# Sort companions moved ahead of the folds, and six gather passes written out, in a graph network kernel

## The reference, cut to what matters

```python
def reference(x, src, dst, edge_type_16, edge_weight, ...):
    edge_index = jnp.stack([src, dst])
    # L0, three times: e = relu((x[dst]-x[src]) @ theta.T + x[src] @ phi.T); segment_max over src; batch norm; relu
    x = _layernorm(x + _L0_gnn_ref(x, src, dst, ...), axis=-1)
    # L1, twice: msg = (x @ W[type])[src] * edge_weight; mean over dst; + x @ root + bias; layer norm; relu
    x = _layernorm(x + _L1_gnn_ref(x, edge_index, edge_type_16, edge_weight, ...), axis=-1)
    # L2: (x @ W)[src] * norm, sum over dst; relu
    x = _layernorm(x + _L2_gnn_ref(x, edge_index, ...), axis=-1)
    # L3: attention along edges with a softmax over dst, then an MLP
    x = _layernorm(x + _L3_gnn_ref(x, src, dst, ...), axis=-1)
    return x
```

## Time and profile before

| | |
|---|---|
| time, median of 3 runs | 7478.22 us (7474.63 to 7485.05) |
| profiled execution | 7499.41 us, span 7497.7 us |
| busy, share of the span | VectorE 3766.1 us (50%), GpSimd 3180.5 (42%), TensorE 3015.6 (40%), ScalarE 1788.8 (24%) |
| moved by DMA | 1065.32 MB, mean 142 GB/s |
| mean granted TensorE clock | 0.691 |

### The profile page before, as it was taken

One profiled execution on the slowest core, in us unless ns is written; L12 is line 12 of the kernel. 1 busy time (PEld: TensorE's weight loads), 2 busy tenths in 40 slices (PEclk: granted clock), 3 DMA queues, 4 the chain that ended last, 5 costly groups with the idle time before them and its releaser, 6 DMA issues. The chain is left out here.

```text
span 7497.7 us, 64492 instructions
## 1 busy us (share of the span) xinstructions
PE 3015.6 (40%) x12777; PEld 1767.9 (24%) x12803; DVE 3766.1 (50%) x9366; ACT 1788.8 (24%) x4594; POOL 3180.5 (42%) x3188
## 2 busy tenths in 40 slices
PE   4373000433335445569700069400030005767748
PEld 3232000311113222234300024200020003555525
DVE  8995444344445455644445343333353335656553
ACT  1282000021112354521122222222220002333312
POOL 0003565434443555410266620366536663555540
PEclk9997555755556677779855579755565557888869
DMA  0003455323332444323355543455535553887840
GB/s 8 1 1 106 162 172 172 116 90 131 123 127 98 137 144 147 137 79 153 139 171 174 171 172 137 145 171 172 177 97 172 179 179 125 269 271 267 271 105 18
DMA packets 379809, 1065.32 MB, mean 142 GB/s; under 512 B 74258, under 2 KB 162612, under 8 KB 333012
## 3 DMA queue, kind: packets, MB, share of 16 engines
q0 software_dynamic: 164688, 466.32, 21.1%
q1 hardware_dynamic: 213586, 595.68, 21.0%
q10 hardware_dynamic: 1330, 0.99, 0.0%
HBM read 541.40 MB, written 521.29 MB: 142 GB/s over the span
## 5 line engine op out<-in xcount | busy, mean ns | idle before, releaser
L788 POOL DMA_INDIRECT out_of<-table,index x936 | 930.5, 994 | 1035.2 <-DVE index L812 756.2
L788 POOL DMA_INDIRECT rows<-table,index x728 | 719.5, 988 | 412.9 <-issue 229.6
L788 POOL DMA_INDIRECT rows<-typed_table,index x520 | 514.0, 988 | 684.4 <-DVE index L812 533.6
L3108 POOL DMA_INDIRECT qv<-qv_table,index x416 | 429.0, 1031 | 384.1 <-DVE index L3285 256.5
L788 POOL DMA_INDIRECT y<-typed_table,index x312 | 321.4, 1030 | 597.8 <-DVE index L812 504.8
L1493 PE MATMUL bank<-x,marks 128*128 128x416 f16 x1664 | 380.4, 386 | 418.9 <-ACT marks L1507 340.6
L827 DVE SCALAR_TENSOR_TENSOR y<-y,by_source_anew,out_of 128x256 f32<-128x256 f32 x897 | 434.0, 484 | 213.4 <-issue 89.4
L1507 ACT ACTIVATE marks<-hot_block,x 128x128 f16<-128x128 f16 x1248 | 370.9, 386 | 436.1 <-DVE marks L1548 430.3
L806 ACT ACTIVATE rows<-rows,by_target_weight 128x256 f32<-128x256 f32 x520 | 215.6, 494 | 611.2 <-DMA rows<-typed_table,index 586.8
L2157 PE MATMUL bank<-weights,turned_y 128*128 128x512 f32 x800 | 359.1, 598 | 5.5 <-ACT turned_y L2217 5.5
L1961 PE MATMUL bank<-weights,out_of 128*128 128x512 f32 x800 | 349.6, 595 | 13.2 <-DVE weights L2006 13.2
(11 more groups left out here) (586 smaller groups left out, 7605.4 us busy)
## 6 DMA issues: line engine op xcount, KB each, us to landing
states<-y SPq DMA_DIRECT2D x156, 1024.0 KB
typed_table<-staged SPq DMA_DIRECT2D x400, 256.0 KB, 2.0
states<-state SPq DMA_DIRECT2D x78, 1024.0 KB
states<-out_of SPq DMA_DIRECT2D x78, 1024.0 KB
wide_states<-y SPq DMA_DIRECT2D x52, 1088.0 KB
near<-k_rows SPq DMA_DIRECT2D x416, 128.0 KB
out_of<-table,index POOLq DMA_INDIRECT x936
rows<-table,index POOLq DMA_INDIRECT x728
```

Of the source, the lines that this page charges most:

```text
L788: pool.indirect_dma_start(out=rows[h][:, u * D:(u + 1) * D], out_offset=None, in_=table, in_offset=bass.IndirectOffsetOnAxis(ap=index[h][: ...
L3108: pool.indirect_dma_start(out=qv[b][:, u * PAIR:(u + 1) * PAIR], out_offset=None, in_=qv_table, in_offset=bass.IndirectOffsetOnAxis(ap=ind ...
```

## The change

- The loops of VectorE, ScalarE, TensorE and SyncE in `edge_pass`, `over_groups` and `Mixture` become Python loops: every group is its own code, slices and semaphore values are constants, and `held` goes. GpSimd's loop stays.
- Each companion has a `lead`: `CountTargets` and `PlaceTargets` 1, `MoveTargets` 3. VectorE does the companion's group g + lead behind `fold_group(g)`.
- `begin` gives the order of round 0: in pass 1 the four folds, the preparation, five companion groups; in pass 2 the settling with the four folds put between its parts, five groups; in pass 3 the preparation, three groups, and then a fold and a group in turn; in pass 6 the folds and then `ahead`, as before.
- `behind` stands before the last fold of the pass.

```diff
-                late = bool(beside) and beside.late
-                if beside and not late:
-                    dve.wait_ge(loaded, 16 * len(loads))
-                    beside.ahead(dve)
                 mixed_rounds = mixing.rounds if mixing else 1
+                if beside:
+                    beside.begin(dve, [lambda h=h: fold_group(0, h) for h in range(RING)])
+                else:
+                    for h in range(RING):
+                        fold_group(0, h, mix=bool(mixing))
+                for i in range(1, rounds - 1):
+                    for h in range(RING):
+                        fold_group(i, h, mix=i < mixed_rounds)
+                        beside_group(i, h)
                 for h in range(RING):
-                    fold_group(0, h, alone=late, mix=bool(mixing))
-                if late:
-                    beside.ahead(dve)
-                    for h in range(RING):
-                        beside.group(dve, h, h % 2)
-                if mixing:
-                    with dve.Fori(1, mixed_rounds) as i:
-                        for h in range(RING):
-                            fold_group(i, h, mix=True)
-                with dve.Fori(mixed_rounds, rounds - 1) as i:
-                    for h in range(RING):
-                        fold_group(i, h)
-                for h in range(RING):
+                    if beside and h == RING - 1:
+                        beside.behind(dve)
                     fold_group(rounds - 1, h, more=False)
+                    if beside and GROUPS - RING + h + beside.lead < GROUPS:
+                        beside_group(rounds - 1, h)
                 dve.wait_ge(chain, STEPS + 1)
                 nc.vector.tensor_copy(tail[:], state[RING - 1][:, (GROUP - 1) * D:])
-                if beside:
-                    beside.behind(dve)
...
-def over_groups(engine, body):
-    for h in range(2):
-        body(h, h)
-    with engine.Fori(1, GROUPS // 2 - 1) as i:
-        for h in range(2):
-            body(2 * i + h, h)
-    for h in range(2):
-        body(GROUPS - 2 + h, h)
+def over_groups(body):
+    for g in range(GROUPS):
+        body(g, g % 2)
...
+# MoveTargets
+    def begin(self, dve, folds):
+        self.ahead(dve)
+        for g in range(self.lead):
+            self.group(dve, g, g % 2)
+        for h, fold in enumerate(folds):
+            fold()
+            self.group(dve, h + self.lead, (h + self.lead) % 2)
...
+# PlaceTargets
+    def begin(self, dve, folds):
+        nc, order = self.sort.nc, self.sort.order
+        nc.vector.tensor_copy(self.run[0][:], order.start[:]).then_inc(self.running, 1)
+        self.settle.vector(dve, folds)
+        self.mask(dve, 0, 0)
+        for g in range(RING + self.lead):
+            self.group(dve, g, g % 2)
```

More of the change, by code:

```diff
@@ L799, in _ @@
                 def _(act):
-                    with act.Fori(0, rounds) as i:
+                    for i in range(rounds):
                         for h in range(RING):
                             act.wait_ge(gathered[h], (i + 1) * (16 * GROUP))
-                            act.sem_inc(held, 1)
                             for u in range(GROUP):
                                 row = rows[h][:, u * D:(u + 1) * D]
-                                nc.scalar.activation(row, row, ACT.Copy, scale=order.weight[:, bass.ds((RING * i + h) * GROUP + u, 1)]
+                                nc.scalar.activation(row, row, ACT.Copy, scale=order.weight[:, (RING * i + h) * GROUP + u:(RING * i + h) * GROUP + u + 1]
                                                      ).then_inc(weighed, 1)
@@ L831, in fold_group, with beside_group @@
                         look(g + RING, h)
-                    if beside and not alone:
-                        beside.group(dve, g, h % 2)
                     if mix:
                         mixing.group(dve, i, h)
+                def beside_group(i, h):
+                    if beside:
+                        beside.group(dve, RING * i + h + beside.lead, (h + beside.lead) % 2)
                 nc.vector.memset(state[RING - 1][:, (GROUP - 1) * D:], start).then_inc(chain, 1)
@@ L883, in _ @@
                     mixing.load(sp)
[L884 to L887, removed]
+                for i in range(rounds):
+                    store(i, mix=bool(mixing) and i < mixing.rounds)
                 if mixing:
@@ L1084 @@
 class CountTargets:
-    late = True
-    names = ("bits_made", "hot", "turned", "copied", "tallied", "summed", "totalled", "held")
+    lead = 1
+    names = ("bits_made", "hot", "turned", "copied", "tallied", "summed", "totalled")
     def __init__(self, sort):
@@ L1129, in body @@
                 act.wait_ge(turned, g + 1)
-                act.sem_inc(held, 1)
-                nc.scalar.copy(sort.z[:, bass.ds(g * P, P)], turn_bank[h][:, 0:P]).then_inc(copied, 1)
-            over_groups(act, body)
+                nc.scalar.copy(sort.z[:, g * P:(g + 1) * P], turn_bank[h][:, 0:P]).then_inc(copied, 1)
+            over_groups(body)
+    def begin(self, dve, folds):
+        for fold in folds:
+            fold()
+        self.ahead(dve)
+        for g in range(RING + self.lead):
+            self.group(dve, g, g % 2)
     def ahead(self, dve):
@@ L1214, in scalar, with vector @@
             nc.scalar.copy(order.end_row[:, b * BLOCK * P:b * BLOCK * P + block_width(b)], env.bank[2 + b % 2][:, 0:block_width(b)]).then_inc(self.kept, 1)
-    def vector(self, dve):
+    def vector(self, dve, folds):
         nc, env, order = self.sort.nc, self.sort.env, self.sort.order
+        first, second, third, fourth = folds
         n_blk, n_stp, l_blk, l_stp, end, crosses = self.n_blk, self.n_stp, self.l_blk, self.l_stp, self.end, self.crosses
@@ L1252, in vector @@
                                     op=ALU.mult).then_inc(self.masked_ends, 1)
+        second()
         dve.wait_ge(self.used, TILES)
@@ L1256, in vector @@
         nc.vector.tensor_scalar(out=self.ident_v, in0=env.ident[:], scalar1=self.open_all[:, 0:1], scalar2=None, op0=ALU.mult).then_inc(self.opened, 1)
+        third()
         dve.wait_ge(self.opened_row, 1)
         then(nc.vector.tensor_copy(order.open_row[:], env.bank[1][:, 0:P]))
+        fourth()
 class PlaceTargets:
-    late = True
+    lead = 1
     names = ("masked", "hot_tile", "alike", "compared", "code_met", "hot_block", "crossed", "hot_row", "tallied", "running", "added",
-             "cut_high", "cut", "looked_up", "picked", "placed", "ranked", "held") + SettleTargets.names
+             "cut_high", "cut", "looked_up", "picked", "placed", "ranked") + SettleTargets.names
     def __init__(self, sort):
@@ L1461 @@
 class MoveTargets:
-    late = False
-    names = ("step", "hot", "marked", "used", "held")
+    lead = 3
+    names = ("step", "hot", "marked", "used")
     def __init__(self, sort):
@@ L2032 @@
 class Mixture:
-    names = ("basis_loaded", "mixed", "filed", "mix_held")
+    names = ("basis_loaded", "mixed", "filed")
     rounds = TYPES // 2
@@ L2061, in group @@
             return
-        first = isinstance(c, int) and c == 0
+        first = c == 0
         if h == 0:
```

128 lines of the change are left out of this document (46 added, 82 removed).

## The result

| | before | after |
|---|---|---|
| median | 7476.43 us (7463.51 to 7485.05, 4 runs) | 7094.62 us (7038.82 to 7144.45, 4 runs) |
| ratio | | 0.9474 (95% interval 0.9438 to 0.9511) |
| profiled span | 7497.7 us | 7142.8 us |
| gathers with waits, passes 1 to 6 | 631, 854, 740, 648, 626, 615 us | 601, 690, 679, 589, 579, 596 us |
| GpSimd's waits in them | 95, 331, 189, 99, 91, 77 us | 51, 159, 109, 39, 42, 52 us |

What follows compares the result with a forecast made beforehand. GpSimd's row gathers, waiting 882 us in all mostly for VectorE's `index`, were taken to bound the kernel. Savings summed to 830 us, 7499 to 6669, set at about 6650 us for the median; 8 in 10 within 6550 to 7000.

Steps and rivals of the forecast that it cites:

- Loops written out: VectorE, ScalarE, TensorE, SyncE: register, branch and `held` instructions go, and with them the slow stretches returning each round.
- pass 1 and its end: Pass 1: waits fall from 95 to 17 us, saving 78; its last store comes 11 us sooner.
- pass 2 and its end: Pass 2: fewer waits save 261 us; no companions left over after the last gather saves 26.
- pass 3 and its end: Pass 3: stretch of 740 us falls to 576, saving 164; the next phase starts 46 us sooner.
- Passes 4 to 6: Last three passes: VectorE's groups well under GpSimd's 10.3 us, so waits nearly vanish, saving 96, 88 and 60 us.
- the first wait: Pass 2's first GpSimd wait, 61.9 us before: settling moved between folds leaves 40 us, bounds 15 to 62.
- the 553 taken: Pass 2's 416 gathers at 1.33 us each, gap included: 553 us.
- 10 us a group: Pass 3's companion through two buffers: 19 to 20 us for two groups, under GpSimd's pace by little.
- The ends: Ends of passes 1 to 3: `behind` before the last fold finds companions done, saving 11, 26 and 46 us.
- Rival B: Written-out code pays for its fetches, VectorE losing 30% of its time: 475 us saved, 7000 us; chance 0.19.
- Rival C: VectorE and GpSimd hinder each other: 2496 gathers each 0.11 us longer, 275 us, so 6925 us; chance 0.13.
- D: Slower than before: all written-out code at 0.70 us an instruction, pass 3's TensorE worst, about 9000 us; chance 0.04.

Runs made afterwards that it cites:

- experiment 6: The changed kernel, unchanged, run for its trace on a chip where the kernel before takes about 6355 us: 6366.05 us, ratio 1.0012.
- experiment 12: The changed kernel plus 24 one-column writes of zeros on VectorE per group in pass 6, on a slow chip: 7145.99 us, ratio 0.9548.
- experiment 5: The kernel before, unchanged, run for its trace on a quick chip: 6350.75 us.
- experiment 1: The kernel before with only the leads, the new round 0 order and the moved `behind`, all loops kept, on a quick chip: 6347.24 us, ratio 0.9983.
- experiment 14: The kernel before with only the loops written out, no lead and `behind` last, on a slow chip: ratio 0.9555.
- experiment 11: The changed kernel with a 128x866 write of zeros on VectorE ahead of each companion group in pass 1, on a slow chip: 7071.76 us, ratio 0.9431.

## Why the prediction was wrong

The mechanism was seen, its cure misjudged, and the gain that came was there on some chips only. **The step that failed is the first of "Loops written out": that the slow stretches go with the loops' register and branch instructions.** They come in straight code too, at the same 0.70 us, and cost 362 us of waits more than the 90 that the forecast left. Term by term, from the profiled executions:

| term | forecast | measured |
|---|---|---|
| pass 1 and its end | 78 + 11 | 30 - 10 |
| pass 2 and its end | 261 + 26 | 164 + 8 |
| pass 3 and its end | 164 + 46 | 61 + 17 |
| pass 4 | 96 | 59 |
| pass 5 | 88 | 47 |
| pass 6 | 60 | 18 |
| everything else | 0 | -39 |

The measured terms come to 355 us, the difference of the two profiled executions; the medians differ by 382.

- *Passes 4 to 6*: a fold went from 4.2 us to 0.7 or 1.4 us within the stretches, not to 0.52. That is 12.5 us a group, above GpSimd's 10.3.
- *Pass 2*: the first wait, taken as 40 us, is 43. Its gathers are 22 us less than the 553 taken (416 times 0.977 + 0.30 = 531); another 116 us of waits stayed.
- *Pass 3*: 10 us a group was about right where the supply is quick (groups 8 to 12 us apart); TensorE's slow stretches add a wait of 9 to 13 us ten times, 110 us.
- *The ends*: `behind` ahead of the last fold makes the last store wait for the companion, and the companion was late for the same reason. On the quick chip the stores lie 6 to 7 us behind the last gather, as forecast.
- *Rival B* had the mechanism, with 475 us for the 382 and too low a chance, though not where it takes its time. It gave passes 1 and 4 to 6 80% of their gain (they kept 154 of 322 us) and pass 3 20 us (it got 61).
- *Rival C*: gathers grew by 51 us over before, but the forecast had taken most of that in; over its 1.29 to 1.36 us a gather they are 7 us longer, not 275. *D* didn't come: stretches end.

What misled me is the earlier trace rows, one view of an engine chosen for a whole stage. The attention pass wasn't free of the slow supply. Waits in a part of it (who, for whom: us, times, longest), in 600 us of before on the first chip, then in 500 us of it on the quick one:

```profile
POOL qv L3108 <- DVE index L3285: 191.6, 20, 14.6
```

```profile
POOL qv L3108 <- DVE index L3285: 80.2, 19, 5.7
```

Between its first and last gather it takes 805 us on the one and 663 on the other. The prediction also misread its rate: the 620 us of the earlier trace rows hold 313 gathers, not the 416 of 52 groups, so a group took 15.5 us there (805 us for 52) and not some 12. I compared it with slower stages instead of with what its engines needed.

The Trainium skill, page "Runtime: NRT & Kernel Launch", section "Instruction fetch mechanics", says that straight code is fetched ahead, mostly hidden. The quick chips agree with it (in experiment 6 VectorE has one idle time over 0.5 us that is put down to "issue", TensorE and ScalarE none); experiment 12's chip doesn't, by the 1.34 us ahead of instructions that wait for nothing. By that rule the time would have been 6608, by the measurement it is 7095. The same section says that a taken branch out of the blocks at hand stalls for a fetch. The quick chips show something of that kind, and small: in pass 2 of experiment 5 TensorE stands 0.52 to 0.57 us at 23 turns of its loop, and at none in experiment 6, where it is written out:

```profile
1457.07 1.03 PE L1300 MATMUL bank<-mine,x 128*128 128x512 bf16 x2 [0.52 <-issue]
```

The trace doesn't tell whether the fetch or the loop's own instructions take it, and hardly any of it reaches GpSimd: in experiment 1, with all its loops, that waits 10 us in pass 2 and 2 to 3 us in each other pass.

What stays open is why one program has two speeds: no run put a chip on both sides, and a load from elsewhere wasn't looked for. The packets of the instruction queues are the same in number and size at both (before and experiment 5: 80 of 16 KB and 131 of 8 KB; after and experiment 6: 105, and 173 or 174) and take about as long (16 KB, median: 1.12 and 1.02 us before, 1.04 and 1.00 after), and a gather takes 0.95 us at both. So it isn't the amount of code fetched that differs.

## What to carry to other kernels

Idle time at one fixed spacing, put down to "issue", is the supply of instructions. Before it is priced as something that a change removes, run the unchanged kernel again on another chip: here 1120 of 7478 us, and all that the change gains, are gone on three of the six. Where an engine is free of such stretches in one stage, look at all its partners there before that stage is taken as the model for new code. And where the gatherer never waits, moving VectorE's work had nothing to win, and by where one operation fell against the gathers it cost 26 us in pass 1.

## What the runs showed of the hardware

- Two speeds of the same program, by chip or session: 6351 to 6356 us and 7352 to 7478 us. At the slow one an engine gets one instruction per 0.70 or 1.40 us for some 10 to some 450 us at a time (experiment 14, pass 5), in loops and in straight code, on VectorE, ScalarE and TensorE; SyncE's loads in the attention pass start 0.7 us apart 63 times in the first trace and never in experiment 5's.
- A gather that starts in the first us of a 1.2 us operation of VectorE with two bf16 inputs lasts until 0.82 us behind its end, so 1.1 to 2.0 us instead of 0.95; one that started just before it (0.12 us) is not held up. The Trainium skill, page "SBUF — State Buffer", section "Who interferes with whom", says that the order of issue decides who blocks; the trace agrees with it in 0.95 against 1.23 us. It also says that an operation of VectorE with at most one input in SBUF, outside the modes that take both ports, doesn't contend with GpSimd. A write of zeros has no input, and the 47 gathers of experiment 11 that started within one took 2.0 to 2.3 us; that speaks against the page if it is the write that held them, and not the two-input operation right behind it. A write that stands alone wasn't run.
